# Second attention of a fused transformer kernel: the next batch's q and k projections and the expert ranks at other steps, and gathers that read their slots directly

## The chip, the cores and the metric

The kernel runs on one core of a Trainium2 chip. The time is the device time of one execution in microseconds (us); lower is better. All data are float32 but for the one-hot and counting operands of the router, which are bfloat16.

## What is computed

Four residual blocks over x of 16 batches, 512 tokens, width 128. Each block begins with a layer norm.

```python
x = x + attention_a(layernorm(x))   # 16 heads of 8; causal linear attention
x = x + ffn(layernorm(x))           # top-2 of 16 experts, capacity CF 1.25
x = x + attention_b(layernorm(x))   # 16 heads of 8
x = x + ffn(layernorm(x))           # the same experts again

def attention_b(x):
    Q, K, V = x @ wq.T + bq, x @ wk.T + bk, x @ wv.T + bv      # by head
    scores = einsum('bhqd,bhkd->bhqk', Q, K) * scale
    top_u = top_k(scores.max(axis=-1), 6)[1]     # 6 queries of a head attend
    ctx = softmax(einsum(Q[top_u], K) * scale) @ V
    return zeros.at[top_u].set(ctx) @ wo.T + bo

def ffn(x):
    w, idx = top_k(softmax(x @ router_w), 2)
    rank = cumsum(one_hot(idx)) - one_hot(idx)   # place within the expert
    # pairs whose rank is under the capacity go through the expert:
    # down(silu(gate(x)) * up(x)), scaled by w and added up by token
```

## The kernel before, in words

x stays in SBUF (`xs`). The program has five stages, each engine's own list of instructions tied to the others by semaphores: attention a over 16 batches, two expert segments (`experts(0)`, `experts(1)`, 24 groups each), attention b over 16 batches, and two expert segments again (`experts(2)`, `experts(3)`). Tokens go to the experts through DRAM by POOL's scattering DMAs (`send`), and come back by POOL's gathering DMAs (`fetch`, 8 a batch) into `yg`, from where DVE adds them to `xs` (`add_choice`, four instructions for each of the two choices: the first combine and the second combine). The change is in attention b and in `fetch`.

**A round.** Attention b is a function `body(b, ...)` on each engine, called for b from 0 to 15; this text calls a call a round. Round b goes through 32 steps (`PAIRS`; step n below is "pair n"). A step is: PE makes two matmuls of scores for two heads into one of three PSUM tiles (`pair`, `scores`, L1814); ACT takes the relu of half of each (L816, two instructions); DVE takes the row maxima (`largest`, L1321, two instructions, each followed by an accumulator read). Three PSUM tiles mean that PE's scores of step n wait for DVE's maxima of step n-3 (semaphore `bmax_done`). After most odd steps PE does some other matmul for batch b-1 (its six chosen queries: `select_x`, `select_q`, `selected_scores`, `turn_exp`, `context_x`, `context`, `context_out`, `scatter_context`), for batch b+1 (`turn`, `project_q`, `project_k`) and for the router of batch b-2 (`turn`, `logits`, `ranks`). ACT and DVE carry the matching pieces after their own step n. Every engine runs its list in order, so a piece stands in front of all later steps of its engine. The steps are written out by hand (`if next and n == 9: project_q(b + 1)`); nothing else sets the order. Rounds 2 to 14 have all pieces (13 rounds); `next` is false in round 15, `before` in rounds 0 and 1.

**Bank 0.** One PSUM bank (`bank[0]`) holds, in turn: the largest scores turned (step 3), the two normalised batches turned (steps 5 and 7), the q projection of batch b+1 (PE step 9, L1797; read by ACT's four `masked_q` copies at steps 9 to 12, L779), its k projection (PE step 17, L1802; read by ACT's `keys` at step 18, L787), and the ranks of batch b-2 (PE step 21, L1558 to L1564; read by DVE's `route_ranks` at step 21, L1020 to L1025). Semaphores: `bproj_done` for q and k, `qm_ready` for the masked q, `bkT_ready` for the keys, `oneh_done` for the one-hot choice (DVE, step 11), `rk_done` for the ranks.

**POOL in a round**, in order: `fetch` for batch b+2 (8 gathers, L522), `selected_rows` (L598), `key_differences` of batch b+1 (L603, waits for the keys), `add_bias` (L530), `places` (nine small instructions, wait for the ranks), `send` (8 scatters, L482), `sent` (waits until they landed), `normed` (L609, L612).

**Gathers.** Their rows come from `slots`, which DVE computes for half of the batches at a time (`table_slots`). Before a fetch DVE copies 8 columns of `slots` to a small buffer (`indices`, L1226, `slg`), and `fetch` waits for that copy (`slg_ready`).

## Time and profile before

| | us |
|---|---|
| median of three runs | 1549.39 |
| lowest and highest | 1541.33, 1552.91 |
| the profiled execution | 1551.83 |
| its span in the profile | 1549.5 |
| PE busy | 1305.2 (84% of the span) |
| DVE busy | 1137.9 (73%) |
| ACT busy | 768.2 (50%) |
| POOL busy | 732.2 (47%) |

The profile shows one execution. The busy time of an engine is the union of its instructions; the share says nothing of which engine is waited for, and this program has stages with different limits. TensorE's granted clock is either 2.4 GHz (1.00 in the profile) or 1.2 GHz (0.50), and a stretch's figure is the mean. The 2.3 us between span and time lie around the profiled instructions. In a row of windows stand the window, its length, the busy time and instructions of PE, PE's weight loads, DVE, ACT and POOL, the mean granted clock, the DMA share and GB/s. In a row in order of time stand start, duration, engine, line, operation, output and inputs, shapes, count, and in brackets the idle time before and what ended it. Matmuls of 32 rows on different row groups overlap, so that four instructions of one pair of steps end nearly together.

### The profile page before, as it was taken

Reading aid. Unit: us, or ns where it says so; the run is one execution under the profiler, and the core shown is the slowest. Engines: PE = TensorE matmul, PEld = TensorE weight load, DVE = VectorE, ACT = ScalarE, POOL = GpSimd, SP = SyncE. Lnnn points to the kernel's source line nnn. Section 1 sums busy time; section 2 is a strip of 40 time slices with the busy share of each in tenths; the row PEclk is TensorE's granted clock in tenths of the full one; section 3 lists DMA queues with packets and bytes.
Section 4 is the critical chain, followed back from the end, with each engine's and each line's share of the span. In section 5 each row is a group of like instructions: output and inputs, shape, how many; then the busy total and the mean of one; then the engine's idle time right before and its main releaser. Section 6 shows DMA issues by size and latency. Waiting matters only on the chain.

```text
span 1549.5 us, 28769 instructions
## 1 busy us (share of the span) xinstructions
PE 1305.2 (84%) x8534; PEld 802.8 (52%) x8534; DVE 1137.9 (73%) x5084; ACT 768.2 (50%) x1903; POOL 732.2 (47%) x1041
## 2 busy tenths in 40 slices
PE   3988888887899999999999999999999989999300
PEld 1555554454798964444444444444444448888300
DVE  3898998898473658788888889888888784755422
ACT  2343443341564766555655656556555556646200
POOL 2135555446423213354555655545554342347775
PEclk9999999999899988888988979978888889999755
DMA  6645412001354520000000000110000003557522
GB/s 171 226 140 176 139 57 75 27 24 55 112 187 155 176 83 14 10 19 26 22 23 28 29 21 21 38 60 28 29 25 18 28 29 121 162 159 229 161 80 70
DMA packets 119770, 125.82 MB, mean 81 GB/s; under 512 B 15552, under 2 KB 109888, under 8 KB 119616
## 3 DMA queue, kind: packets, MB, share of 16 engines
q1 hardware_dynamic: 103232, 90.42, 18.2%
q0 software_dynamic: 16384, 33.59, 7.5%
q8 instruction: 68, 1.11, 0.3%
q14 instruction: 86, 0.70, 0.2%
HBM read 50.15 MB, written 73.79 MB: 80 GB/s over the span
## 4 chain that ended last, share of the span: by engine, by line
PE 49%; DVE 27%; issue 7%; POOL 7%; ACT 5%; DMA 3%; SPq 1%; POOLq 0%; ACTq 0%; DVEq 0%
PE pair L1814 19%; DVE pT L1321 7%; PE pair L1741 7%; POOL vmyg L522 5%; DVE pT L1047 3%; PE pair L1752 3%; DVE xs L1231 3%; PE pair L1730 2%; PE pair L1605 2%; ACT pT L816 2%; PE bank L1544 2%; PE bank L1550 2%; PE bank L1842 2%; DVE st L898 2%; PE bank L1802 1%
## 5 line engine op out<-in xcount | busy, mean ns | idle before, releaser
L1814 PE MATMUL pair<-kT,apart 32*128 32x512 f32 x2048 | 480.6, 743 | 34.7 <-DVE smax L1321 33.4
L816 ACT ACTIVATE pT<-pair 128x256 f32<-128x256 f32 x1024 | 328.9, 396 | 259.0 <-PE pair L1814 257.5
L1321 DVE CUSTOM_DVE_ANT_0 pT<-pair,pT 128x256 f32<-128x256 f32 x1024 | 381.4, 417 | 100.9 <-ACT pT L816 97.4
L1814 PEld LDWEIGHTS pair<-kT,apart 32*128 32x128 f32 x2048 | 196.0, 210 | 194.7 <-DVE smax L1321 118.9
L1741 PE MATMUL pair<-xeT,unit_w 128*128 128x256 f32 x768 | 186.9, 387 | 0.0
L1047 DVE TENSOR_TENSOR pT<-pair,causal 128x512 f32<-128x512 f32 x256 | 158.4, 680 | 23.8 <-PE pair L1605 23.8
L522 POOL DMA_INDIRECT vmyg<-ybufA,slg x128 | 122.3, 955 | 84.9 <-issue 36.6
L1206 DVE TENSOR_TENSOR hid<-sg,pair 128x512 f32<-128x512 f32 x96 | 65.9, 686 | 126.3 <-ACT sg L742 125.9
L1741 PEld LDWEIGHTS pair<-xeT,unit_w 128*128 128x128 f32 x768 | 142.0, 195 | 16.0
L482 POOL DMA_INDIRECT dispB<-xnf,sli x128 | 126.5, 988 | 43.6 <-issue 43.6
L482 POOL DMA_INDIRECT dispA<-xnf,sli x128 | 126.9, 992 | 40.6 <-issue 40.6
L1231 DVE SCALAR_TENSOR_TENSOR xs<-vmyg,wts,xs 128x128 f32<-128x128 f32 x256 | 84.7, 391 | 81.8 <-DMA vmyg<-ybufB,slg 63.1
L522 POOL DMA_INDIRECT vmyg<-ybufB,slg x128 | 122.5, 957 | 41.8 <-issue 39.8
L1752 PE MATMUL pair<-unit_w,hid 128*128 128x128 f32 x768 | 102.2, 276 | 9.2 <-DVE ye L1214 9.1
L1752 PEld LDWEIGHTS pair<-unit_w,hid 128*128 128x128 f32 x768 | 99.6, 191 | 17.6 <-DVE hid L1206 11.8
L749 ACT ACTIVATE unit_w<-f_w 128x384 f32 x160 | 74.9, 515 | 52.8 <-PE pair L1752 48.3
L1605 PE MATMUL pair<-apart,kT 32*128 32x512 f32 x512 | 75.1, 656 | 18.6 <-DVE pT L1047 18.6
L603 POOL TENSOR_TENSOR kT<-kT 128x256 f32<-128x256 f32 x16 | 11.7, 731 | 156.4 <-ACT kT L787 156.4
L557 POOL COPY vmyg<-tok 128x128 f32<-128x128 f32 x64 | 16.9, 295 | 144.4 <-DVE tok L1039 108.6
L742 ACT ACTIVATE sg<-pair 128x512 f32<-128x512 f32 x96 | 57.4, 598 | 54.0 <-PE pair L1741 53.7
L1321 DVE DVE_READ_ACCUMULATOR2_ANT smax<- 128x1 f32 x1024 | 83.2, 81 | 0.0
L1629 PE MATMUL bank<-pT,vmyg 128*32 128x128 f32 x2048 | 73.4, 287 | 0.0
(235 smaller groups left out, 2025.8 us busy)
## 6 DMA issues: line engine op xcount, KB each, us to landing
dispB<-zeros SPq DMA_DIRECT2D x16, 1408.0 KB
apart<-dispA SPq DMA_DIRECT2D x96, 128.0 KB
ybufA<-ye SPq DMA_DIRECT2D x48, 256.0 KB
apart<-dispB SPq DMA_DIRECT2D x96, 128.0 KB
ybufB<-ye SPq DMA_DIRECT2D x48, 256.0 KB
dispA<-zeros SPq DMA_DIRECT2D x33, 128.0 KB
xs<-in_x SPq DMA_DIRECT2D x16, 256.0 KB, 3.0
out<-xs SPq DMA_DIRECT2D x16, 256.0 KB, 2.5
```

The source lines that it names most:

```text
L482: pool.indirect_dma_start(out=area, out_offset=bass.IndirectOffsetOnAxis(ap=sli[h][:, K * j + k:K * j + k + 1], axis=0), in_=xnf[h][:, j, ...
L522: pool.indirect_dma_start(out=yg[h][:, j, :], out_offset=None, in_=ybuf[second(g)], in_offset=bass.IndirectOffsetOnAxis(ap=slg[h][:, j:j + ...
L749: last = act.activation(unit_w[g % NX][:, u, :], f_w[:, bass.ds(ex[u], 1), :].rearrange("p a n -> p (a n)"), ACT.Copy)
L816: act.activation(rel[n % RING][:, q, :], pair[n % RING][:, q, HALF:SEQ], ACT.Relu).then_inc(s["relu_done"], 1)
L1047: dve.tensor_tensor(pT[n % (2 * NG)][:, :, :], bank[4 + n % 4].rearrange("p (j t) -> p j t", j=GH), causal[:, :].unsqueeze(1).to_broadcast ...
L1231: last = dve.scalar_tensor_tensor(out=xb, in0=yg[h][:, K * j + k, :], scalar=wts[:, bass.ds((b * TB + j) * K + k, 1)], in1=xb, op0=ALU.mul ...
L1321: dve.tensor_tensor_reduce(out=rel[n % RING][:, q, :], in0=pair[n % RING][:, q, 0:HALF], in1=rel[n % RING][:, q, :], scale=1.0, scalar=LOW ...
L1605: pe.matmul(bank[4 + g][:, :].rearrange("p (j t) -> p j t", j=GH), kTs[h][at, c * P:(c + 1) * P], apart[h][at, :, c * P:(c + 1) * P], star ...
L1629: last = pe.matmul(bank[1][at:at + QG, c * P:(c + 1) * P], vm[:, c, j * P + at:j * P + at + QG], pT[c % 2 * NG + g][:, j, :], start=(c == ...
L1741: last = pe.matmul(bank[3 + 2 * h + k][:, u * UR:(u + 1) * UR], unit_w[r][:, u, k * D:(k + 1) * D], xeT[h][:, UT * u:UT * (u + 1), :].rear ...
L1752: last = pe.matmul(bank[7][:, j * D:(j + 1) * D], hid[h][:, j, :], unit_w[r][:, j // UT, 2 * D:3 * D], start=True, stop=True)
L1814: pe.matmul(pair[n % RING][:, q, :], apart[h][at, j, t * P:(t + 1) * P], kTs[h][at, HALF:], start=True, stop=True).then_inc(s["bsc_done"], 1)
```

## The change

- PE: `project_q` goes from step 9 to step 17, `project_k` from 17 to 23 (after `context`), `ranks` from 21 to 14. In a round that has ranks, `project_q` now first waits for DVE's `route_ranks` (`rk_done`), since both use bank 0; `ranks` waits for the copy of the turned batch (`att_xT_ready`) and no longer for the keys.
- ACT: the four `masked_q` copies go from steps 9 to 12 to steps 18 to 21, `keys` from 18 to 24.
- DVE: `route_ranks` goes from step 21 to 16. The `indices` copies go (32 in the program), and the last step of `table_slots` raises `slots_in` and is no longer waited for on DVE.
- POOL: the gathers read `slots`; a fetch waits for `slots_in` (first two of each half) and for the combine of two batches before. `key_differences` stands behind `add_bias`, `places` and `send`.

```diff
             def fetch(g, h):
-                pool.wait_ge(s["slg_ready"], g + 1)
+                if g % HALFB in range(2):
+                    pool.wait_ge(s["slots_in"], g // HALFB + 1)
+                if g > 1:
+                    pool.wait_ge(s["combined"], g - 1)
...
-                        in_offset=bass.IndirectOffsetOnAxis(ap=slg[h][:, j:j + 1], axis=0),
+                        in_offset=bass.IndirectOffsetOnAxis(ap=slots[:, at + j:at + j + 1], axis=0),
...
# POOL, body
-                if next:
-                    key_differences(b + 1, 1 - h)
                 add_bias(b, b + B, b_bo)
                 if before:
                     places(b - 2, b - 2 + B, h)
                     send(b - 2 + B, u - 1 + B // 2, h)
+                if next:
+                    key_differences(b + 1, 1 - h)
+                if before:
                     sent(u - 1 + B // 2, h)
...
# ACT, body
-                    if next and 9 <= n < 13:
-                        masked_q(b + 1, 1 - h, range(n - 9, n - 8))
+                    if next and 18 <= n < 22:
+                        masked_q(b + 1, 1 - h, range(n - 18, n - 17))
...
-                    if next and n == 18:
+                    if next and n == 24:
                         keys(b + 1, 1 - h)
...
# DVE
-                    link(dve.tensor_scalar(slots[:, cols], shift[:, cols], float(ZROW), None, ALU.add))
+                    dve.tensor_scalar(slots[:, cols], shift[:, cols], float(ZROW), None, ALU.add).then_inc(s["slots_in"], 1)
...
-                    if fetch and n == 1:
-                        indices(b + 2, h)
...
-                    if before and n == 21:
+                    if before and n == 16:
                         route_ranks(b - 2 + B, bank[0])
...
# PE, body
-                    if next and n == 9:
-                        project_q(b + 1)
...
+                    if before and n == 14:
+                        if next:
+                            pe.wait_ge(s["att_xT_ready"], b + B + 2)
+                        else:
+                            pe.wait_ge(s["ffn_xT_ready"], b + B - 1)
+                        ranks(b - 2 + B, bank[0])
...
                     if next and n == 17:
-                        project_k(b + 1)
+                        if before:
+                            pe.wait_ge(s["rk_done"], b + B)
+                        project_q(b + 1)
...
+                    if next and n == 23:
+                        project_k(b + 1)
```

How PE's list reads from step 10 on, in round 4. Before (the scores are `pair<-kT,apart`, x4 for two steps; `xnT,b_wq` is the q projection, `xnT,b_wk` the k projection, `kT,qsel` the selected scores):

```order
L1797 MATMUL bank<-xnT,b_wq 128x512
L1814 MATMUL pair<-kT,apart 128x512 x4
L1833 MATMUL bank<-pT,xnb 128x128 x4
L1814 MATMUL pair<-kT,apart 128x512 x4
L1838 MATMUL bank<-xsel,b_wq 128x128
L1814 MATMUL pair<-kT,apart 128x512 x4
L1842 MATMUL bank<-kT,qsel 128x512
L1814 MATMUL pair<-kT,apart 128x512 x4
L1802 MATMUL bank<-xnT,b_wk 128x512
L1814 MATMUL pair<-kT,apart 128x512 x4
```

After, from `select_q` on (the five rows of `onesb` and `before` are the ranks):

```order
L1829 MATMUL bank<-xsel,b_wq 128x128
L1805 MATMUL pair<-kT,apart 128x512 x2
L1549 MATMUL bank<-ohsum,onesb 128x128
L1552 MATMUL bank<-oneh,onesb 128x96
L1552 MATMUL bank<-oneh,onesb 128x64
L1552 MATMUL bank<-oneh,onesb 128x32
L1555 MATMUL bank<-oneh,before 128x128
L1805 MATMUL pair<-kT,apart 128x512 x2
L1833 MATMUL bank<-kT,qsel 128x512
L1805 MATMUL pair<-kT,apart 128x512 x4
L1788 MATMUL bank<-xnT,b_wq 128x512
L1805 MATMUL pair<-kT,apart 128x512 x4
```

The q projection has left its place ahead of steps 10 and 11 and stands where the k projection stood; the ranks part the scores of step 14 from those of step 15.

ACT's list around the same place of round 4. Before, from `selected_exp` on (step 17):

```order
L791 ACTIVATE pT,asum<-bank,aneg 128x512
L816 ACTIVATE pT<-pair 128x256 x2
L787 ACTIVATE kT<-bank,cols 128x512
L816 ACTIVATE pT<-pair 128x256 x2
L800 ACTIVATE pT<-bank 128x512
L816 ACTIVATE pT<-pair 128x256 x4
L810 ACTIVATE xctx<-bank 128x128
```

After:

```order
L796 ACTIVATE pT,asum<-bank,aneg 128x512
L821 ACTIVATE pT<-pair 128x256 x2
L784 ACTIVATE apart<-bank,qbias,inturn 128x512
L821 ACTIVATE pT<-pair 128x256 x2
L784 ACTIVATE apart<-bank,qbias,inturn 128x512
L805 ACTIVATE pT<-bank 128x512
L821 ACTIVATE pT<-pair 128x256 x2
L784 ACTIVATE apart<-bank,qbias,inturn 128x512
L821 ACTIVATE pT<-pair 128x256 x2
L784 ACTIVATE apart<-bank,qbias,inturn 128x512
L815 ACTIVATE xctx<-bank 128x128
```

Four masked copies of q now stand between the relus of steps 18 to 22, where one copy of the keys stood.

## Rows read from the trace of the kernel before

**Rows 1.** Windows: rounds 2 to 14 together.
```profile
648.10:1239.50 591.40, 553.03 (x2570) 262.64 (x2570) 495.86 (x2682) 345.75 (x1015) 315.02 (x400) 0.87 0.09 28
```

**Rows 2.** POOL in order of time: first and last of the 128 gathers at the end.
```profile
1380.12 1.31 POOL L522 DMA_INDIRECT vmyg<-ybufA,slg  x1 [8.61 <-DMA ybufA<-ye]
...
1542.00 0.95 POOL L522 DMA_INDIRECT vmyg<-ybufB,slg  x1 [0.30 <-issue]
```

**Rows 3.** The largest wait of DVE, rounds 2 to 14: us in total, times, longest.
```profile
DVE pT L1321 <- ACT pT L816: 74.2, 82, 2.5
```

**Rows 4.** Windows: round 8, round 12, and two stretches of round 12.
```profile
920.50:963.10 42.60, 40.09 (x198) 20.41 (x199) 36.93 (x205) 26.40 (x79) 24.10 (x31) 0.91 0.09 26
...
1102.10:1149.00 46.90, 43.39 (x199) 20.11 (x199) 38.41 (x207) 26.54 (x78) 24.64 (x33) 0.86 0.08 23
...
1116.00:1119.40 3.40, 2.01 (x8) 1.01 (x9) 3.33 (x18) 2.50 (x9) 2.18 (x2) 0.97 0.14 41
1119.40:1126.20 6.80, 6.80 (x16) 1.89 (x14) 3.56 (x18) 1.58 (x6) 0.00 (x0) 0.51 0.01 2
```

**Rows 5.** PE in round 8, in order of time: start, duration, idle before.
```profile
929.62 1.12 PE L1797 MATMUL bank<-xnT,b_wq 128*128 128x512 f32 x2
...
938.74 1.14 PE L1814 MATMUL pair<-kT,apart 32*128 32x512 f32 x8
939.81 1.13 PE L1802 MATMUL bank<-xnT,b_wk 128*128 128x512 f32 x2
940.87 1.40 PE L1814 MATMUL pair<-kT,apart 32*128 32x512 f32 x8
...
948.03 0.49 PE L1858 MATMUL bank<-xctx,b_wv 128*128 128x128 f32 x2
948.45 1.93 PE L1814 MATMUL pair<-kT,apart 32*128 32x512 f32 x8
...
958.49 4.58 PE L1814 MATMUL pair<-kT,apart 32*128 32x512 f32 x16 [1.47 <-DVE smax L1321]
```

**Rows 6.** DVE in round 8: steps 10, 16, the two combines, 18, ranks, 22, 24.
```profile
932.25 0.42 DVE L1321 CUSTOM_DVE_ANT_0 pT<-pair,pT 128x256 f32<-128x256 f32 x1 [1.18 <-ACT pT L816]
...
940.32 0.42 DVE L1321 CUSTOM_DVE_ANT_0 pT<-pair,pT 128x256 f32<-128x256 f32 x1 [0.59 <-ACT pT L816]
...
941.70 1.14 DVE L1231 SCALAR_TENSOR_TENSOR xs<-vmyg,wts,xs 128x128 f32<-128x128 f32 x4
942.75 0.42 DVE L1321 CUSTOM_DVE_ANT_0 pT<-pair,pT 128x256 f32<-128x256 f32 x1
...
944.26 1.98 DVE L1231 SCALAR_TENSOR_TENSOR xs<-vmyg,wts,xs 128x128 f32<-128x128 f32 x4
...
947.92 0.28 DVE L1020 TENSOR_TENSOR rkoh<-bank,oneh 128x128 f32<-128x128 f32 x1
...
948.44 0.41 DVE L1321 CUSTOM_DVE_ANT_0 pT<-pair,pT 128x256 f32<-128x256 f32 x1
...
950.08 0.41 DVE L1321 CUSTOM_DVE_ANT_0 pT<-pair,pT 128x256 f32<-128x256 f32 x1
```

**Rows 7.** ACT in round 8: a masked copy, the next two relus, the turned exponentials.
```profile
932.37 0.78 ACT L779 ACTIVATE apart<-bank,qbias,inturn 128x512 f32<-128x512 f32 x1
933.03 0.67 ACT L816 ACTIVATE pT<-pair 128x256 f32<-128x256 f32 x2
...
943.67 0.63 ACT L800 ACTIVATE pT<-bank 128x512 f32<-128x512 f32 x1
```

**Rows 8.** POOL in round 8: bias, first scatter; in round 12 POOL beside DVE's one-hot.
```profile
944.03 1.27 POOL L530 TENSOR_TENSOR xs<-xs,b_bo 128x512 f32<-128x512 f32 x1
...
950.98 1.10 POOL L482 DMA_INDIRECT dispA<-xnf,sli  x1 [0.64 <-issue]
...
1116.61 1.62 POOL L598 TENSOR_SCALAR pT<-tokrow,idc 128x512 f32<-128x512 f32 x1
...
1116.74 0.81 DVE L993 TENSOR_TENSOR oneh<-eiota,topf 128x64 bf16<-128x64 f32 x2
```

More of the change, by code:

```diff
@@ L157, in build @@
         sli = [sb(f"sli{h}", [P, TB * K], I32) for h in range(2)]
-        slg = [sb(f"slg{h}", [P, TB * K], I32) for h in range(2)]
         vmyg = sb("vmyg", [P, TB * GH * (D + DH)])
@@ L238, in build @@
                  "xe_in0 xe_in1 xe_tp xeT_ready unit_w_ready gu_done silu_done hid_done y_done y_ready xe_in2 xe_in3 y_out0 y_out1 "
-                 "slg_ready got0 got1 comb0 combined "
+                 "slots_in got0 got1 comb0 combined "
                  "n_done q_done k_done kv_done einv_ready qT_ready turns_ready kT_ready lefts past_done stats2 unit_w_act tok_ready vm_ready pv_done sc_done pT_ready state_done stm_ready ctxT_ready o_done "
@@ L517, in fetch @@
             def fetch(g, h):
-                pool.wait_ge(s["slg_ready"], g + 1)
+                if g % HALFB in range(2):
+                    pool.wait_ge(s["slots_in"], g // HALFB + 1)
+                if g > 1:
+                    pool.wait_ge(s["combined"], g - 1)
                 settle(pool)
+                at = (g % B) * TB * K
                 for j in range(TB * K):
@@ L1222, in experts @@
                 y_copy(G - 1)
-            def indices(b, h):
-                dve.tensor_copy(slg[h][:, :], slots[:, bass.ds(b * TB * K, TB * K)]).then_inc(s["slg_ready"], 1)
             def add_choice(b, h, k, done, tiles=range(TB)):
@@ L1280, in chain_a @@
                     table_slots(0, (g - 12,))
-                if g == 15:
-                    indices(0, 0)
-                    indices(1, 1)
                     dve.wait_ge(s["w_in2"], 16 * 11)
@@ L1509, in pieces @@
                     table_copy(3, bank[0])
-                if g == 19:
-                    indices(0, 0)
-                    indices(1, 1)
             def add_all(b, parts=range(2)):
@@ L1521, in add_all @@
                     add_choice(b, h, 1, s["combined"], range(TB))
-                    if b + 2 < B:
-                        indices(b + 2, h)
             EARLY = (GRP - 4) // 3
@@ L1704, in table_rows @@
             def table_rows(seg, at):
-                pe.wait_ge(s["tb"], (11, 22, 45, 62)[seg])
+                pe.wait_ge(s["tb"], (11, 22, 43, 59)[seg])
                 for n, src in enumerate((trow, texpc)):
@@ L1912, in body @@
                     if next and n == 17:
-                        project_k(b + 1)
+                        if before:
+                            pe.wait_ge(s["rk_done"], b + B)
+                        project_q(b + 1)
                     if last and n == 19:
                         turn_exp(b - 1)
-                    if before and n == 21:
-                        if next:
-                            pe.wait_ge(s["bkT_ready"], b + 2)
-                        else:
-                            pe.wait_ge(s["ffn_xT_ready"], b + B - 1)
-                        ranks(b - 2 + B, bank[0])
                     if last and n == 21:
@@ L1933, in body @@
                         pe.wait_ge(s["rk_done"], b + B)
+                        pe.wait_ge(s["bkT_ready"], b + 2)
                         if b == MID + 1:
```

## The prediction

> **What bounds the kernel now.** I read the busy time by stage first, then the waits of the stage that changes, then one of its rounds engine by engine. The end is set by POOL: its 128 gathers run without a pause from 1380.12 to 1542.95 us, and they begin when the stores of the third expert segment have landed [rows 2]. What comes before 1380 is a chain of stages, so a microsecond won or lost in attention b moves the start of the gathers, and the end, by one. Rounds 2 to 14 last 591.4 us, 45.5 each [rows 1]. In them DVE works 495.9 us and is idle 95.5, or 7.3 a round; 74.2 us of that wait for ACT's relus [rows 3]. ACT is busy for only 345.8 us of the 591.4 [rows 1]; it is mostly PE's scores that come late behind another matmul, or at the half clock. So the round is a loop: maxima of step n-3 on DVE, scores on PE, relu on ACT, maxima of step n. A piece on PE is free as long as DVE has a piece of the same length at the same place.
>
> The rounds differ by the clock. Round 8 takes 42.6 us at a mean granted clock of 0.91, round 12 takes 46.9 at 0.86 [rows 4]. In round 12 PE is busy for 2.01 of the 3.40 us from 1116.0, and then the clock stands at 0.51 for the 6.8 us from 1119.4. Round 8 has no such stretch in its middle, so I work the change out on its rows.
>
> **Step 10: a gain.** The q projection starts at 929.62 and lasts, like k, 1.06 us to the next matmul (939.81 to 940.87). It holds the scores of steps 10 and 11 back by that, and DVE waits 1.18 us for the relu of step 10 at 932.25 [rows 5, 6]. Without it DVE starts step 10 near 931.20, 1.05 earlier (DVE's own piece ahead leaves 0.13 of the wait). The pieces up to step 16 shift with it: step 16 starts at 939.27 and not at 940.32. The ranks on PE in between take about 0.2 us and fall where PE waits for DVE's long choice of step 11; I cost them at nothing. If that cover were gone they would cost their 0.2.
>
> **Step 17: the new wait.** The q projection now waits for `rk_done`. A step's maxima take 0.69 (940.32 to 941.70 is two steps), so those of step 16 end at 939.27 + 0.69 = 939.96. The ranks take 0.52 (947.92 to 948.44), so PE starts q at about 940.56 where k began at 939.81 [rows 5, 6]. Since the scores of steps 16 and 17, begun at 938.74 before and at 937.69 now, end 1.07 later near 938.7, PE stands still for 1.86 us, and the scores of steps 18 and 19, and the rest of its list, stand behind that wait. Then q 1.06, the scores 1.07 (938.74 to 939.81), and from the scores' end to DVE's start 0.51 (939.81 to 940.32): step 18 starts at 943.20. DVE meanwhile has step 17 (0.69) and the first combine (1.05, 941.70 to 942.75), so it is ready at 942.22 and waits 0.98. Before, step 18 began at 942.75. The gain of 1.05 is spent; the 0.52 of ranks is only done earlier.
>
> **Steps 18 to 22: ACT's queue.** A masked copy keeps ACT for 0.66 us (932.37 to 933.03), two relus for about 0.54 (0.67 with the part that overlaps the next), the turned exponentials for about 0.47 of their 0.63 [rows 7]. From the first relu of step 18 (942.77) on: relus to 943.31, copy 943.97, relus 944.51, copy 945.17, exponentials 945.64, relus 946.18, copy 946.84, relus 947.38, copy 948.04, context copy about 948.2, and then the relus of step 22. DVE's step 22 starts at 948.6; before it was 948.44 [rows 6].
>
> The second combine hides part of this. It takes 1.98 us where the first takes 1.14, and POOL's bias add lies over it, 944.03 to 945.30 [rows 6, 8]. The bias add leaves that place because it no longer stands behind the keys. That is up to 0.84 on DVE, but the walk above is ACT's, and DVE waits for it anyway. The bias add also arrives next to the one-hot choice, whose two instructions took 0.81 under POOL's row selection in round 12 [rows 8]. I count nothing for the move, with bounds of 0.84 saved and 0.8 lost. The Trainium skill (GPSIMD Engine Reference, section Architecture) says that GpSimd's SBUF read port is shared with DVE. By that rule the collision moves with the bias add and the sum stays as it is; by the two rows alone it might vanish, and a round would win up to 0.84.
>
> **Step 23: k.** PE does the context (0.42, 948.03 to 948.45), then k (1.06), then the scores of 24 and 25 (1.07), and 0.51 to DVE: 3.06 in all [rows 5]. Its start lies between 948.3 (the context copy on ACT is ready) and 948.8 (the scores of step 23, if the second combine still ends late), so DVE starts step 24 between 951.3 and 951.9. Before it was 950.08 [rows 6]. DVE has only 0.26 us of its own there. So the round is 1.2 to 1.8 late there, and the rest of it keeps its distances, since DVE's rows stand close together after that. The saving on the second combine speaks for the lower end: I take 1.4 a round.
>
> **The rest.** `key_differences` on POOL goes behind eight scatters. The first scatter stood 2.5 after the end of the ranks (948.44 to 950.98, [rows 6, 8]) and would now go at 943.0; eight of them at no more than 1.4 end by 954.2, and the next round's scores come after 958.5 [rows 5]. I cost it at nothing. If it came later than that, every round would start late by the difference. The 32 copies of indices go: about 0.07 us each on DVE, 13 of them in these rounds, 0.9 us. The gathers at the end wait for a combine that is two batches back; they are 1.25 us apart now and will be after [rows 2].
>
> **The sum.** 13 rounds x 1.4 = 18.2, less 0.9, is 17.3. 1551.8 for the profiled execution plus 17.3 is 1569.1. The median of the three runs stands 2.4 below that execution, so 1566.7; I say 1567. A measurement of this kernel tells about 1%, 15.5 us, from no change.
>
> **Rivals.**
> *The clock gets better (0.15).* The stretch at 0.51 in the middle of a round follows a gap in PE's work around steps 12 to 15. If spreading q and k takes these stretches away, a round falls from the mean 45.5 to the 42.6 of round 8, plus 1.4: 13 x 1.5 = 19.5 less than before, 1530. It decides if PE's busy share before step 16 rises. For it: 4.3 us lie between rounds 8 and 12, and the price is real. Against it: the change takes PE's work out of the steps just before that gap and adds a gap of 1.86 us.
>
> *The clock gets worse (0.20).* The new gap of 1.86 us is longer than the 1.47 us at 957.0 [rows 5], and a stretch at half clock lies under q, the scores, the exponentials. At half clock q and the scores behind it take 2.1 us more. If this happens in every second or every round beyond what there is now, 7 to 13 x 2.1 = 15 to 27 comes on top: 1582 to 1594, say 1586. The Trainium skill (TensorE: Matmul & The Clock Gate, section Why this matters for your kernels) warns of idle gaps that are longer than any here; by it the clock would stay up and this rival would be worth nothing. Row and rule differ: at 1119.4 the clock is down after a stretch in which PE was busy for 2.01 of 3.40 us [rows 4].
>
> *It cancels (0.25).* The bias add leaves the second combine and meets nothing, the gain at step 10 holds, and the late steps find cover: k's context starts at its early bound, and the 0.84 counts in full against step 24. Then a round gains 1.05 and 0.84 and loses 0.98 and 1.2 less the 0.26 of DVE's own piece, about zero: 1549, where the saved waits and the new ones are of one size. For it: ACT is busy for only 345.8 of 591.4 us. Against it: the walk has ACT's four copies in front of the relus just where the 0.84 would be won.
>
> My forecast has 0.40. The range that holds the time in 8 of 10 cases runs from 1530, the first rival's centre, to 1588, a little over the second's. Faster by over 1%: 0.17 (the first rival and a little of the third). Slower by over 1%: 0.43 (the clock's 0.20 and over half of my own case, whose centre lies only 2 us over the bound). The same: 0.40.
>
> **What would show it.** In the profile after: rounds 2 to 14 last 610 us. DVE's wait of 1.18 us at pair 10 has gone; a wait of about 1 us stands before pair 18 and one of 1.3 us or more before pair 24; PE is idle for nearly 1.9 us ahead of the q projection, released by the ranks. The second combine takes under 2 us. POOL's key differences end long before the next round's first scores. I am wrong if step 18 starts without a wait, or if the mean clock of the 13 rounds moves from 0.87 by more than 0.02: 4.3 us part the rounds at 0.91 and 0.86 [rows 4], so 0.01 of it is worth up to 0.9 us a round.

## The result: slower, by more than forecast

The changed kernel takes 1590.77 us (median of 4 runs, 1586.13 to 1593.93), the kernel before 1545.36 (1532.03 to 1552.91); the ratio is 1.0301, 95% interval 1.0221 to 1.0381. The forecast was slower, 1567, with 1588 as the upper end of the range: the direction was right, 18 us were expected and 45 came. Executions that stood over 1.5% above the fastest of their kernel are left out of all ratios, while the medians given in this text take them in.

The chain at the end is what it was. The first gather starts at 1418.43 where it started at 1380.12 [rows 2], 38.3 later, and the span has grown by 38.0 (1549.5 to 1587.5). POOL in order of time, kernel after:

```profile
1418.43 1.00 POOL L526 DMA_INDIRECT vmyg<-ybufA,slots  x1 [7.98 <-DMA ybufA<-ye]
```

So the time lies ahead of the gathers. The windows of the kernel after: rounds 2 to 14, round 8, round 13, and two stretches of round 8. The columns are those of [rows 1].

```profile
641.72:1278.35 636.63, 552.02 (x2567) 255.72 (x2566) 500.66 (x2667) 341.61 (x1015) 319.19 (x400) 0.84 0.09 26
936.62:987.04 50.42, 44.03 (x198) 19.57 (x198) 38.53 (x205) 26.28 (x78) 24.77 (x32) 0.80 0.07 22
1189.62:1232.70 43.08, 37.57 (x198) 18.12 (x197) 37.62 (x211) 26.42 (x79) 26.01 (x34) 0.97 0.09 26
948.60:952.20 3.60, 2.42 (x14) 0.73 (x13) 3.56 (x17) 2.06 (x7) 3.21 (x3) 1.00 0.07 22
952.60:967.60 15.00, 12.87 (x36) 4.29 (x36) 8.50 (x43) 4.98 (x14) 4.96 (x11) 0.54 0.03 9
```

The 13 rounds take 636.6 us, 45 more than the 591.4 of [rows 1]; the rest of the program gives 7 back. PE has the same busy time (552), DVE works 5 us more and stands idle 136.0 instead of 95.5. The clock is 0.84, it was 0.87. There are two kinds of round: at a clock of 0.97 the new order needs 43.08 us, next to the 42.6 at 0.91 of [rows 4], but rounds 2 to 11 all take between 47.7 and 54.2, at 0.72 to 0.89. Round 8, with 50.42 at 0.80 and a mean clock of 0.54 for 15 us in its middle, is one of the longer ones; in rounds 2, 3, 5 and 7 the clock is down for less of the middle, and they take 47.7 to 48.9.

The waits of rounds 2 to 14, in total, times, longest; first those of DVE (against [rows 3]), then those of PE:

```profile
DVE pT L1319 <- ACT pT L821: 117.7, 119, 3.4
DVE amax L1351 <- PE bank L1833: 9.6, 9, 1.2
...
PE bank L1788 <- DVE rank L1030: 23.3, 13, 1.8
PE bank L1549 <- DVE oneh L998: 12.4, 8, 1.7
```

The q projection waits 1.8 us for the ranks in each of the 13 rounds: that was forecast. New and not forecast is the last line: PE waits in 8 rounds, 1.55 us each, for DVE's one-hot of the router's choice, a wait that the kernel before doesn't have. The groups of DVE show why (busy, mean ns, idle before), first the kernel before, then the kernel after:

```profile
L1231 DVE SCALAR_TENSOR_TENSOR xs<-vmyg,wts,xs 128x128 f32<-128x128 f32 x96 | 37.3, 449 | 0.0
L993 DVE TENSOR_TENSOR oneh<-eiota,topf 128x64 bf16<-128x64 f32 x26 | 6.1, 276 | 0.2
...
L1232 DVE SCALAR_TENSOR_TENSOR xs<-vmyg,wts,xs 128x128 f32<-128x128 f32 x96 | 27.3, 346 | 0.0
L998 DVE TENSOR_TENSOR oneh<-eiota,topf 128x64 bf16<-128x64 f32 x26 | 19.0, 768 | 0.2
```

The combines lay under POOL's bias add before, and the one-hots lie under it now. The add has left the second combine, which gives 10.0 us back, and has come to the one-hots, which now take 12.9 us more. Round 8 in order of time, POOL, DVE, PE:

```profile
949.01 1.60 POOL L602 TENSOR_SCALAR pT<-tokrow,idc 128x512 f32<-128x512 f32 x1
950.57 1.27 POOL L534 TENSOR_TENSOR xs<-xs,b_bo 128x512 f32<-128x512 f32 x1
...
950.04 2.02 DVE L998 TENSOR_TENSOR oneh<-eiota,topf 128x64 bf16<-128x64 f32 x2
...
952.22 0.22 PE L1549 MATMUL bank<-ohsum,onesb 128*128 128x128 bf16 x1 [1.19 <-DVE oneh L998]
952.27 0.25 PE L1552 MATMUL bank<-oneh,onesb 128*128 128x96 bf16 x3
952.37 0.22 PE L1555 MATMUL bank<-oneh,before 128*128 128x128 bf16 x1
952.94 2.38 PE L1805 MATMUL pair<-kT,apart 32*128 32x512 f32 x4 [0.36 <-DVE smax L1319]
```

The two one-hots, 0.35 us together elsewhere, end only at 952.06, just behind the bias add at 951.84. PE has stood for 1.19 us, and its next scores run at the half clock. A ninth round is held like this, though the wait for the one-hots doesn't show it: in round 6 DVE is past the one-hots when the bias add comes (852.99 to 854.28). The add stops another small operation, the maxima of step 12 come late, and PE waits for those:

```profile
852.70 1.61 DVE L1007 SCALAR_TENSOR_TENSOR sbase<-topf,kbase 128x8 f32<-128x8 f32 x1
...
854.71 2.41 PE L1805 MATMUL pair<-kT,apart 32*128 32x512 f32 x4 [1.82 <-DVE smax L1319]
```

That round takes 50.2 us. And here is what stands in round 8, 8 us behind its one-hots, at the q projection, and beside it round 13, where nothing collided.

```profile
961.14 2.08 PE L1788 MATMUL bank<-xnT,b_wq 128*128 128x512 f32 x2 [1.79 <-DVE rank L1030]
965.67 0.42 DVE L1319 CUSTOM_DVE_ANT_0 pT<-pair,pT 128x256 f32<-128x256 f32 x1 [2.85 <-ACT pT L821]
...
1201.63 0.35 DVE L998 TENSOR_TENSOR oneh<-eiota,topf 128x64 bf16<-128x64 f32 x2
1203.25 1.59 POOL L602 TENSOR_SCALAR pT<-tokrow,idc 128x512 f32<-128x512 f32 x1
1208.75 1.12 PE L1788 MATMUL bank<-xnT,b_wq 128*128 128x512 f32 x2 [1.79 <-DVE rank L1030]
1211.38 0.42 DVE L1319 CUSTOM_DVE_ANT_0 pT<-pair,pT 128x256 f32<-128x256 f32 x1 [0.95 <-ACT pT L821]
1212.60 0.42 DVE L1319 CUSTOM_DVE_ANT_0 pT<-pair,pT 128x256 f32<-128x256 f32 x1 [0.44 <-ACT pT L821]
1216.90 0.42 DVE L1319 CUSTOM_DVE_ANT_0 pT<-pair,pT 128x256 f32<-128x256 f32 x1 [0.61 <-ACT pT L821]
1219.50 0.43 DVE L1319 CUSTOM_DVE_ANT_0 pT<-pair,pT 128x256 f32<-128x256 f32 x1 [0.87 <-ACT pT L821]
```

The wait of PE is 1.79 in both. At the half clock the q projection takes 2.08 instead of 1.12 and DVE waits 2.85 before step 18 instead of 0.95. Summed over the rows of DVE's timeline in rounds 2 to 14, its idle time before step 18 grows from 3.0 us to 27.6. (Sums by step below come from such rows too.)

### The profile page after: what moved, and what is told of

It reads as the page before. It is cut to its first block and busy times, and to the rows that moved or that the text cites. A ratio compares the mean times of both kernels' runs of the same rounds, so it can differ in the third digit from the quotient of the medians.

```text
span 1587.5 us, 28750 instructions
## 1 busy us (share of the span) xinstructions
PE 1296.7 (82%) x8534; PEld 792.8 (50%) x8534; DVE 1138.8 (72%) x5056; ACT 763.4 (48%) x1903; POOL 735.4 (46%) x1041
## 5 line engine op out<-in xcount | busy, mean ns | idle before, releaser
L1805 PE MATMUL pair<-kT,apart 32*128 32x512 f32 x2048 | 467.1, 751 | 33.1 <-DVE smax L1319 32.0
L1805 PEld LDWEIGHTS pair<-kT,apart 32*128 32x128 f32 x2048 | 184.1, 214 | 175.5 <-DVE smax L1319 97.2
L526 POOL DMA_INDIRECT vmyg<-ybufA,slots x128 | 122.2, 955 | 54.2 <-issue 36.9
L526 POOL DMA_INDIRECT vmyg<-ybufB,slots x128 | 121.9, 952 | 41.9 <-issue 40.4
L1232 DVE SCALAR_TENSOR_TENSOR xs<-vmyg,wts,xs 128x128 f32<-128x128 f32 x256 | 72.9, 346 | 80.2 <-DMA vmyg<-ybufB,slots 63.3
L613 POOL TENSOR_TENSOR xnf<-xs,rstd 128x512 f32<-128x512 f32 x16 | 16.6, 1039 | 152.3 <-DVE nmr L943 152.3
```

The costliest lines, as they stand in the source:

```text
L526: pool.indirect_dma_start(out=yg[h][:, j, :], out_offset=None, in_=ybuf[second(g)], in_offset=bass.IndirectOffsetOnAxis(ap=slots[:, at + j ...
L1232: last = dve.scalar_tensor_tensor(out=xb, in0=yg[h][:, K * j + k, :], scalar=wts[:, bass.ds((b * TB + j) * K + k, 1)], in1=xb, op0=ALU.mul ...
L1805: pe.matmul(pair[n % RING][:, q, :], apart[h][at, j, t * P:(t + 1) * P], kTs[h][at, HALF:], start=True, stop=True).then_inc(s["bsc_done"], 1)
```

## The experiments

Theory A, after the result: the bias add on top of the one-hots stops DVE, then PE, and the clock goes down behind it. Theory B: the moves on TensorE themselves (q behind the ranks, k at 23) cost the time. Theory C: the wait in front of q brings the clock down.

The runs were made in groups, each on one chip with the kernel before beside it, on four chips. On two of them the kernel before takes about 1544 us, as in the result; they are called the first kind below. On the other two, the second kind, it takes about 1787. Medians are compared within one chip where nothing else is said; across chips the ratios to the kernel before are used.

**The whole change again, on both chips of the first kind.** Its two runs are the measure for what was run beside them. Beside the first ran q back at 9, the useless products, and the late bias add in the kernel before; beside the second ran the other three.

> The changed kernel as it is, run beside the others. The first four experiments ran on a chip on which the kernel before takes 1787 us and not 1545, so their ratios (1.003, 1.000, 1.055, 1.032) need this one beside them. Placement theory: the ratio here is 1.03 to 1.05 on either kind of chip. If the ratio on the slow chip is near 1.03, moving the bias add behind the scatters (1.055) cost about 2% and the ranks at step 15 (1.032) changed nothing; if it is near 1.05, the ranks at step 15 won 2%.

1601.67 us (1570.37 to 1609.43, 4 runs) beside 1543.89 for the kernel before. One of the four took 1570.37 and the other three from 1600.28 up, so that this run has no ratio and can't carry a comparison of some 10 or 20 us.

> The changed kernel itself, again, as the measure for the three beside it on whatever chip they get. Every theory expects about 1.03 times before (1590 us where before takes 1545). On the chip where before took 1787 us the steps of the second attention already wait for other reasons; should this chip be like that one, the ratio may be another, and it is then the one that the bias-late and ranks-at-15 runs are to be held against.

1588.52 us (1575.55 to 1605.78) beside 1544.61 for the kernel before, ratio 1.0268 (1.0212 to 1.0324). Its profile holds both kinds of round in one execution. Windows: a round in the middle, and two of the last four.

```profile
938.98:989.45 50.47, 43.57 (x199) 20.10 (x198) 38.62 (x204) 26.11 (x78) 24.87 (x32) 0.80 0.08 22
1086.89:1131.23 44.34, 38.82 (x198) 19.26 (x198) 37.08 (x209) 26.23 (x80) 25.39 (x33) 0.92 0.09 25
...
1175.50:1218.54 43.04, 37.54 (x199) 18.11 (x198) 37.56 (x210) 26.41 (x79) 25.98 (x34) 0.97 0.09 26
```

In the round at 1175.50 the one-hots start at 1187.50, ahead of POOL's product at 1189.10. In the profile rounds 2 to 9 are held and rounds 10 to 14 are not, so the collision seems to repeat until a round of another length breaks it. PE waits for the one-hots 7 times in this profile (1575.55 us), 8 times in the one above (1589.72) and 10 times in that of the other run (1609.43). That the number of such rounds makes this kernel's spread of 30 us is likely; three profiles don't show it.

**Only the bias add moved, on the changed kernel.** This separates A from B and C.

```diff
-                add_bias(b, b + B, b_bo)
                 if before:
                     places(b - 2, b - 2 + B, h)
                     send(b - 2 + B, u - 1 + B // 2, h)
+                add_bias(b, b + B, b_bo)
                 if next:
                     key_differences(b + 1, 1 - h)
```

> The changed kernel with only GpSimd's bias add put behind the scatters, before the key differences. Collision theory: the one-hot operations go back to 0.28 us each, the wait of TensorE before the selected scores and the half-clock stretch that starts there go, 1575 or below against 1590 of the changed kernel (ratio to before 1.015 to 1.02). Rival, from the run on the slow chip (1.055 with the bias add at the very end, where the changed kernel was not run beside it): the later bias add meets the end of the round, where the next round's statistics wait for it, and the run is slower than the changed kernel, 1.04 or more. Third: no difference, the clock falls by the wait for the q projection alone.

1551.71 us (1542.37 to 1556.75, 11 runs), ratio 1.0027 (1.0002 to 1.0052), beside 1588.52 and 1.0268 (1.0212 to 1.0324) of the changed kernel: 36.8 us come back, and the intervals lie far apart. Rounds 2 to 14 of its profile, the one-hots in them, and PE's wait:

```profile
641.82:1238.33 596.51, 526.10 (x2568) 247.14 (x2567) 484.06 (x2670) 341.48 (x1014) 320.37 (x401) 0.88 0.09 27
...
L998 DVE TENSOR_TENSOR oneh<-eiota,topf 128x64 bf16<-128x64 f32 x26 | 4.6, 220 | 0.2
...
PE bank L1788 <- DVE rank L1030: 23.3, 13, 1.8
```

The one-hots take 220 ns, PE's wait for them has gone, and the clock is 0.88. The wait for the ranks is all there, 23.3 us as in the changed kernel. So C by itself is out: with this gap and without the collision the mean clock of the 13 rounds is no lower than it was before the change. B is left with 4 us by the ratio, 7 by the medians, over the kernel before.

**The moves on TensorE taken back, the collision left in.** First q alone, then q and k:

```diff
-                    if next and n == 17:
-                        if before:
-                            pe.wait_ge(s["rk_done"], b + B)
+                    if next and n == 9:
                         project_q(b + 1)
```

with the masked q at 9 to 12 again, the ranks behind `qm_ready` and k at 23 behind `rk_done`.

> The changed kernel with the q projection and its masked copies back at steps 9 to 12; k stays at 23, its copy at 24, the ranks at 14 and 16, POOL's order and the gathers stay. Placement theory, by part: the wait before step 18 goes (27.6 us over 13 rounds), those before 19 and 22 go (13), the one before step 10 comes back (13); k at 23 keeps its 11 us at step 24. So about 25 us less than the changed kernel, ratio 1.010 to 1.018 against before. If the one-hot collision and k were the cause, the ratio would stay at the changed kernel's.

1573.84 us (1563.59 to 1576.07), ratio 1.0161 (1.0099 to 1.0224), where the changed kernel has 1.0301 in the result and 1.0268 above. The intervals touch, so a gain is likely but not clear. Then k at 17 and its eviction at 18:

> The changed kernel with the q projection and masked q back at 9 to 12 and now also the k projection back at 17 and its eviction back at 18: of the moves on TensorE only the ranks at 14 are left. Theory (k at 23 costs by itself): the run with k at 23 showed VectorE waits of 7.1 us before step 22, 10.5 before step 24 and 3.4 more than before at step 28; without k there, 24 and the surplus at 28 go, 14 us, so 1574 becomes 1560 (ratio 1.010), and the 12 or so us left over before are the bias add on top of the one-hot operations. Rival (k is free, VectorE only catches up there with TensorE, which was going to be late anyway): 1570 to 1576, the waits move to steps 19 to 23. Second rival (the ranks at 14 are worth something by themselves): under 1545.

1580.43 us (1573.20 to 1586.01), ratio 1.0212 (1.0167 to 1.0257), beside 1588.52 of the changed kernel. Taking k back gained nothing, and my expectation of 1560 was wrong: DVE's waits before steps 22 and 24 did fall, from 7.1 and 10.5 us to 1.8 and 3.3, but 26.1 us came up before step 18, where there had been none, since k now waits for the ranks at 17. Of the moves on TensorE only the earlier ranks are left here, and 36 us over the kernel before are still lost. Its one-hots and the conversion ahead of them (L993) in rounds 2 to 14:

```profile
L993 DVE CAST topf<-top8i 128x8 f32<-128x8 uint32 x13 | 11.5, 882 | 0.0
L998 DVE TENSOR_TENSOR oneh<-eiota,topf 128x64 bf16<-128x64 f32 x26 | 9.0, 387 | 0.1
```

With q back ahead of it, DVE comes later to this place, and the bias add lies over the conversion instead, 11.5 us where the kernel before has 4.3. Then the same kernel with the bias add behind the scatters, by the diff above:

> The kernel of the run before, with GpSimd's bias add put behind the ranks' bookkeeping and the scatters, before the key differences. Collision theory (the bias add behind the 1.6 us product holds VectorE's one-hot up to 1.9 us, TensorE then waits, and its clock falls in the middle of the round): the mid-round half-clock stretch goes and this run is 8 to 15 us faster than the run before, 1545 to 1550 (ratio 1.00). Rival (the order on GpSimd doesn't matter, as adding the bias late to the kernel before gave 0.9975 only): within 3 us of the run before.

1556.27 us (1548.64 to 1565.53, 11 runs), ratio 1.0061 (1.0030 to 1.0092). 24.2 us come back by the same edit, and the conversions take 3.1 us. It stands 4.6 above the run with all moves and the late bias add, so q at 17 and k at 23 together cost nothing that shows against q at 9 and k at 17. The two profiles also tell what ACT's four masked copies do at steps 18 to 21. Before step 22 DVE waits 7.9 us over the 13 rounds with them there, 1.4 with them at 9 to 12. ACT's relus of steps 22 and 23, with the copies at 18 to 21 (round 13 of the kernel after), where ACT has had no pause since the relus of step 18, and with the copies at 9 to 12 (round 4 of this run):

```profile
1216.37 1.32 ACT L821 ACTIVATE pT<-pair 128x256 f32<-128x256 f32 x4
...
764.55 1.21 ACT L821 ACTIVATE pT<-pair 128x256 f32<-128x256 f32 x4 [0.77 <-PE pair L1805]
```

**The bias add late in the kernel before.**

```diff
                 if next:
                     key_differences(b + 1, 1 - h)
-                add_bias(b, b + B, b_bo)
                 if before:
                     places(b - 2, b - 2 + B, h)
                     send(b - 2 + B, u - 1 + B // 2, h)
+                add_bias(b, b + B, b_bo)
+                if before:
                     sent(u - 1 + B // 2, h)
```

> The kernel before with the bias add behind the scatters, where POOL waits for their landing, so that it meets neither the second combine nor the one-hot choice. Port theory: the second combine takes 1.1 and not 1.9 us in 12 rounds, 10 us less DVE work; 5 to 12 us faster, ratio 0.992 to 0.998. If POOL's additions at the end of the round stop DVE's statistics there instead, 1.00 or more.

1539.99 us (1535.72 to 1548.25, 10 runs), ratio 0.9975 (0.9945 to 1.0004). The second combine goes from 1.98 to 1.14 us here too, 27.2 us for all of them, and this is worth about 4 us by the medians; the interval of the ratio just reaches no change at all. It also gives the price of everything else in the change, with the bias add in the same place in both: 1551.7 - 1540.0 = 11.7 us by the medians, which come from two chips, and 8 us by the two ratios.

**The wait in front of q filled with work.** Three products that nothing reads stand in front of the wait:

```diff
                         if before:
+                            pe.wait_ge(s["bmax_done"], 2 * (b * PAIRS + 15) + 2)
+                            for _ in range(3):
+                                pe.matmul(pair[0][:, 0, 0:2 * P], b_wq[:, :], xnT[:, 0:2 * P], start=True, stop=True)
                             pe.wait_ge(s["rk_done"], b + B)
```

> The changed kernel with three matmuls of no use (128x256, about 0.5 us each at the full clock) on PE between the scores of step 17 and the wait for the ranks, into the tile that step 18 then overwrites; they fill the gap of 1.8 us. Clock theory (the gap lets the clock fall and that doubles the loss at step 18): the mean clock of rounds 2 to 14 rises and the time falls by 10 to 25 us against the changed kernel, ratio 1.015 to 1.025. Placement theory: no less than the changed kernel, or up to 10 us more, since at the half clock the fill lasts longer than the gap.

1575.21 us (1570.74 to 1582.15), ratio 1.0202 (1.0141 to 1.0262), beside 1601.67 (1570.37 to 1609.43) of the changed kernel, whose ratios were 1.0301 and 1.0268 elsewhere. All these intervals overlap: that the useless work makes the kernel faster isn't shown by the times. Rounds 2 to 14 and what PE still waits for:

```profile
639.01:1260.77 621.76, 557.24 (x2646) 269.42 (x2645) 500.51 (x2673) 341.94 (x1015) 320.35 (x401) 0.87 0.09 26
...
PE bank L1549 <- DVE oneh L998: 12.8, 9, 1.8
...
PE bank L1788 <- DVE rank L1030: 2.2, 8, 0.3
```

The collision is untouched, 12.8 us, while the wait in front of q has shrunk from 23.3 us to 2.2 and DVE's wait before step 18 from 27.6 to 14.2. The other profile of the changed kernel has 24.6 there, a clock of 0.86, and 13 rounds of the same 622 us, with fewer rounds held. The fairer measure is the six rounds that are held in all three profiles (2 to 5, 7 and 8): they take 292.6 us with the products, 295.0 and 297.9 without. That the second gap keeps the clock down once the first has brought it down fits these rows, but they are one profile with the products against two without, and don't show it.

**The second kind of chip.** These parts and variants ran on the chips on which hardly anything collides, and where the changed kernel itself was not run. The gathers without the copies of indices, on the kernel before (`slots` read directly):

> The kernel before with one part of the change: the gathers read the slots directly, no index copies, one wait less per slot table. All steps of the second attention stay. Every theory: no change that can be measured. The copies are about 5 us of DVE work in rounds 2 to 14 (4.8 in the trace), so 1540 to 1546 against 1545. If it were slower by more than 1%, the gathers themselves would be a cause that no theory has.

1791.76 us, ratio 1.0033 (1.0008 to 1.0058): nothing, or a third of a per cent lost. POOL's order alone on the kernel before, three times:

> The kernel before with POOL's new order alone: bias add before places and send, key differences behind them. Port theory (POOL's bias add stops DVE's one-hot choice): the one-hot rows grow from 6 to about 19 us over rounds 2 to 14, the second combine loses about 10, PE has a longer gap ahead of step 14 and the clock falls more often; 1550 to 1570. Placement theory (q, k and their masked copies at the wrong steps cost it all): no change, 1545. Clock theory: as the port theory, with the mean clock of the 13 rounds going from 0.87 to 0.84 or 0.85.

> The kernel before with GpSimd's order alone changed as in the changed kernel (bias add right behind the product, key differences behind the scatters), this time on whatever chip the others of this call get. If the collision costs by itself: one-hot operations over 1 us in many rounds, 1565 to 1580 (ratio 1.015 to 1.025). If it costs only together with the moves on TensorE (in the kernel before, the one-hot may come just before or after the bias add, and step 10's wait shifts it): ratio 1.00 to 1.005, as on the slow chip (1.0000).

> The kernel before with GpSimd's order alone changed as in the changed kernel. On a chip on which before takes about 1545 us: 1565 to 1580 (1.015 to 1.025), with one-hot operations over 1 us in many rounds, if the collision costs by itself; 1.00 to 1.005 if it needs the moves on TensorE, which bring the one-hot to the same moment as the bias add. On the chip on which before takes 1788 us: 1.000 again.

Ratios 1.0000 (0.9980 to 1.0019), 0.9987 (0.9963 to 1.0011) and 0.9988 (0.9966 to 1.0010). The bias add stands right behind the product as in the changed kernel, but the one-hots come when both are over. POOL and DVE in the third of them:

```profile
861.68 1.59 POOL L598 TENSOR_SCALAR pT<-tokrow,idc 128x512 f32<-128x512 f32 x1
863.24 1.26 POOL L530 TENSOR_TENSOR xs<-xs,b_bo 128x512 f32<-128x512 f32 x1
...
865.40 0.36 DVE L994 TENSOR_TENSOR oneh<-eiota,topf 128x64 bf16<-128x64 f32 x2
```

So the order does no harm where the two don't meet; whether it would do it alone on a chip of the first kind was not tested. The changed kernel with the order of before:

> The changed kernel with GpSimd's order as before: key differences, bias add, then the ranks' bookkeeping and the scatters. If the 0.75 us of the key differences between the product and the bias add are enough for the one-hot to slip through: 1550 to 1557, like the run with the bias add behind the scatters (1551.7), and all of the 37 us lie in the swap of two small operations. If any bias add near the one-hot holds it: 1575 to 1590, like the changed kernel.

> The changed kernel with GpSimd's order as before (key differences, bias add, bookkeeping, scatters). On a chip on which before takes about 1545 us: 1550 to 1557 (1.003 to 1.008) if the 0.75 us of the key differences between the 1.6 us product and the bias add let the one-hot through; 1575 to 1590 (1.02 to 1.03) if any bias add near the one-hot holds it. On the chip on which before takes 1788 us: 1.016 again.

1819.94 and 1824.50 us, ratios 1.0163 (1.0113 to 1.0214) and 1.0188 (1.0146 to 1.0231). My expectation had the mechanism wrong: the key differences don't put 0.75 us between product and bias add, they wait for the keys of step 24 (19 to 26 us a round in the traces), and the bias add and the scatters wait behind them. In the kernel before it is the same with the keys of step 18: in round 8 the product ends near 935, the key differences wait 8.35 us, and the bias add comes at 944.03 [rows 8]. That wait is what had kept the bias add away from the one-hots. Three more changes to the changed kernel:

```diff
-                    if before and n == 16:
+                    if before and n == 15:
                         route_ranks(b - 2 + B, bank[0])
```

> The changed kernel with DVE's route_ranks one step earlier, at step 15 behind the selected maximum and ahead of step 16's wait. The q projection then need not wait for step 16's maxima. Placement theory: PE's idle of 1.8 us ahead of q goes to about 0.5, DVE's wait before step 18 shrinks by about 1 us a round, and the ranks' 0.52 hide in the 0.59 wait of step 16: 13 to 20 us less, 1570 to 1577. Port theory: no change, 1590. Clock theory: more than 20 us less, since the long gap that lets the clock fall is gone, below 1570.

1838.27 us, ratio 1.0317 (1.0259 to 1.0375). The bias add at the end of POOL's queue, behind the key differences, twice:

> The changed kernel with one POOL instruction moved: the bias add goes behind send and the key differences. Port theory: one-hot rows back to 6 us, the second combine stays short, so 13 us and the clock stretch behind the one-hot gap are won: 1560 to 1575 against 1590. Placement theory: 1585 to 1590. The wait of DVE before step 18 (27.6 us over 13 rounds now) falls towards 13 if half of it is the clock.

> The changed kernel with the bias add at the very end of GpSimd's queue, behind the key differences (which since the change wait for the k eviction of step 24). If this place is bad by itself (the add then starts after step 24 and the output that the end of the round adds to the same rows, and the statistics behind it, wait for it): 1.02 or more above before. If only the slow chip made it so: like the run with the add in front of the key differences, ratio 1.003.

Ratios 1.0548 (1.0484 to 1.0612) and 1.0572 (1.0530 to 1.0615). And the late bias add together with the three useless products:

> The changed kernel with the bias add behind the scatters and three useless 128x256 products of TensorE in front of the wait for the ranks before the q projection. Clock theory: the idle 1.8 us there is what still lets the clock fall in some rounds; filled, the rounds at a clock of 0.82 to 0.88 become 43 us rounds, 1535 to 1545, 7 to 15 us below the run without them. Rival (the wait itself counts, not the clock, and the products only take its place): 1550 to 1556.

1857.77 us, ratio 1.0392 (1.0344 to 1.0439). No one-hot is held in any of these (218 to 220 ns), and they lose 3 to 6% all the same, at clocks of 0.72 to 0.77 in the rounds. Since the gathers and POOL's order alone cost next to nothing here, what is left are the moves on TensorE, alone or together with these and with the place of the bias add. The nearest run on the first kind, the late bias add without the products, lost 0.3%. The reason stays open.

## Why the prediction was right and wrong

**Right: the bound, and the loop.** The gathers start 38.3 us later and the end follows.

**Right: step 10.** DVE's idle time before it falls from 14.4 us to 0.8 over the rounds.

**Right, at full clock: the new wait at 17.** Forecast were 1.86 us of PE and 0.98 of DVE before step 18; round 13 has 1.79 and 0.95.

**Right: ACT's queue.** From the start of step 18 to that of step 22 the walk has 5.4 us (943.20 to 948.6); round 13 has 5.52 (1211.38 to 1216.90), with waits of 0.44 us before step 19 and 0.61 before step 22. The one before step 22 comes with the masked copies: it is 7.9 us in 13 rounds with them at 18 to 21, both in the changed kernel and with the late bias add, and 1.8 and 1.4 in the two runs that have them at 9 to 12 and wait about as long before step 18. That DVE has less of its own in between (0.84 of combine, 0.52 of ranks) is the same in these runs, so it only turns the saved work into a wait.

**k at 23: right in kind, too dear.** 0.87 us of wait before step 24 in round 13 where the signs asked for 1.3 or more. The run with k back at 17 gained nothing, since the wait for the ranks moved with it.

**The term of all the moves** was 17.3 us; 8 to 12 is what the two runs with a late bias add leave for it. The mechanism holds and was sized too high. The 0.9 us for the copies of indices was too small a term: in rounds 2 to 14 eleven of them take 4.8 us, 438 ns each and not 70. Their going showed no gain where it was run alone.

**The step that failed: "I count nothing for the move" of the bias add.** Its saving came as bounded (10.0 us on the combines over the rounds, 0.77 a round). Its loss was bounded at 0.8 a round, from a row in which the one-hots lay under POOL's product, a TENSOR_SCALAR. The bias add is a TENSOR_TENSOR and stands right behind the product: in a collided round the one-hots take 1.67 us more than the 0.35 that they need. The row of the combine under the bias add, 1.98 for 1.14 [rows 6], would have given 0.84 and so about the same bound; no row of before has a small operation under both. And I priced DVE's time alone, not who waits for the one-hots: PE, which stands 1.55 us there and then gets the half clock. Moving the bias add alone gives back 36.8 of the 43.9 us that the changed kernel loses beside it, by the medians. Round 8 and round 13 of the changed kernel tell how: PE is busy for 44.03 us in the one and for 37.57 in the other, for the same 198 instructions.

The Trainium skill (GPSIMD Engine Reference, section Architecture) has the port between SBUF and GpSimd shared with DVE. The trace agrees, with 2.02 us for two one-hots. I had drawn from it that the collision moves and the sum stays. It moved, but the new place is on PE's path and the old was not.

**The rival "the clock gets worse"** was given 0.20 and 1586, and this is what came: 0.84 in the rounds where 0.87 was, past the 0.02 at which the prediction called itself wrong. Its place was only half right. With q's wait in full and the late bias add the mean clock stays at 0.88, so it is the wait for the one-hots behind which it falls; that q's wait then keeps it down is likely and not shown. The Trainium skill (TensorE: Matmul & The Clock Gate, section Why this matters for your kernels) warns of gaps longer than any seen here. By it the clock would have stayed up; the trace has it at 0.54 for 15 us behind gaps of 1.19 and 0.36 us, with the 1.79 us in the middle of that stretch, and the measurement decides.

## What to carry to other kernels

When an instruction is moved on an engine that nobody waits for, look at what it will run beside, not only at what it waits for; the wait removed may have been what kept two operations apart. Price such a meeting by the longest run of operations that the held one can fall under, and follow the held instruction to the engine that waits for it. Where rounds come in two kinds in one trace, compare one of each before adding up averages.

## What the runs showed of the hardware

- POOL's TENSOR_TENSOR of 1.27 us holds DVE's small operations on SBUF to its end (one-hots at 2.02 us for two instead of 0.35, conversions of up to 1.52 instead of 0.14 in the run with k at 17, one of 128x8 elements at 1.61 instead of 0.15). Behind the start of the TENSOR_SCALAR of 1.60 us they go on after about 1 us (949.01 to 950.04 in round 8). DVE's reductions over the scores keep their 0.42 us beside both.
- Gaps of PE of 1.2 to 1.8 us, none over 2, go with a clock of 0.80 in one round where another has 0.97, and with 6.5 us more of PE's busy time for the same instructions. The wait of 1.8 us at q alone, once in each round, goes with a mean clock of 0.88, where the kernel before has 0.87.
- The kernel before takes 1544 us on two chips and 1787 on two others, with the same durations of one operation. On the second kind DVE stands idle where the profile shows nothing to wait for. In its waits this line exists, while the kernel before has none like it in the result's profile (second kind, POOL's order alone, 640 to 1317 us):

```profile
DVE pT L1322 <- issue: 46.9, 52, 3.5
```

  Nearly all of these gaps lie beside POOL's gathers and scatters. Which of the two causes the other, and why the chips differ, stays open.
